# Attention and expert kernel: where slot 0's products on zeros stand, and where two additions of the front stand

## What is computed

```python
x = x + xattn(layernorm(x), ctx)      # 8 batches, 256 channels, 512 positions, 16 heads of 16 channels
x = x + ffn(layernorm(x))             # 2048 tokens of 512 numbers

# xattn
q = Wq @ x + bq; k = Wk @ c + bk; v = Wv @ c + bv
p = softmax(einsum('bhkt,bhks->bhts', q, k) * SCALE)
out = Wo @ einsum('bhts,bhks->bhkt', p, v) + bo

# ffn
h = rmsnorm(x) * rms_weight
probs = softmax(h @ router_w)                     # 8 experts, top 2 kept, their weights made to sum to 1
moe = sum over the two: weight * ((silu(h @ w_gate) * (h @ w_up)) @ w_down)
sh = (silu(h @ sw_gate) * (h @ sw_up)) @ sw_down  # the shared expert, for every token
return moe + sh
```

## Time and profile before

| | |
|---|---|
| device time, median of 3 runs | 826.72 us (823.37 to 827.68) |
| the profiled execution | 826.63 us on the device, span 824.8 us |
| TensorE matmul busy | 779.6 us (95%) |
| VectorE busy | 547.7 us (66%) |
| ScalarE busy | 419.8 us (51%) |
| GpSimd busy | 364.5 us (44%) |
| granted TensorE clock, mean | 0.993 of full |

### The profile page before, as it was taken

How to read it: one execution, slowest core, us unless ns; L and a number is a source line. 1 busy time by engine, 2 the same in 40 slices (tenths; PEclk the granted TensorE clock), 3 DMA queues, 4 the chain that set the end, 5 groups by cost and what they waited for, 6 DMA issues and landing times. The chain is left out here.

```text
span 824.8 us, 11865 instructions
## 1 busy us (share of the span) xinstructions
PE 779.6 (95%) x3879; PEld 393.6 (48%) x3879; DVE 547.7 (66%) x1048; ACT 419.8 (51%) x800; POOL 364.5 (44%) x309
## 2 busy tenths in 40 slices
PE   7999999989999999999999999998999999999993
PEld 3433334334334343343343455775546666666662
DVE  6687898898888888888888767587653223223231
ACT  2124667767768777687776674310343333333331
POOL 4154227417429246173222421000138777777774
PEclk9999999999999999999999999999999999999998
DMA  8959275567565765666543235510946665666553
GB/s 290 216 148 198 62 164 139 115 131 153 126 150 125 157 154 125 132 149 154 116 99 122 94 105 196 238 52 25 340 119 103 94 98 97 102 99 99 90 96 45
DMA packets 54186, 109.67 MB, mean 133 GB/s; under 512 B 12200, under 2 KB 27304, under 8 KB 49888
## 3 DMA queue, kind: packets, MB, share of 16 engines
q1 hardware_dynamic: 37080, 79.39, 38.5%
q0 software_dynamic: 16960, 29.37, 18.8%
q10 hardware_dynamic: 88, 0.16, 0.1%
HBM read 67.90 MB, written 40.86 MB: 132 GB/s over the span
## 5 line engine op out<-in xcount | busy, mean ns | idle before, releaser
L1090 DVE TENSOR_REDUCE negmax<-front_ps 128x1 f32<-128x512 f32 x512 | 326.9, 684 | 68.6 <-PE front_ps L932 67.4
L824 ACT ACTIVATE probs<-st_ps 128x512 f32<-128x512 f32 x512 | 284.0, 598 | 139.4 <-PE st_ps L968 139.1
L1376 POOL DMA_INDIRECT out<-ring,row_i x78 | 123.1, 1578 | 62.5 <-ACT ring L1432 46.4
L1607 PE MATMUL big_ps<-w_gu,attn 128*128 x244 | 111.3, 593 | 0.8 <-ACT attn L1425 0.8
L656 POOL CAST early<-early 128x512 fp32r<-128x512 f32 x28 | 17.1, 612 | 162.3 <-ACT early L772 158.1
L968 PE MATMUL st_ps<-stacks 50*128 50x512 f32 x256 | 68.5, 493 | 2.2 <-ACT probs L824 2.0
L1359 POOL DMA_INDIRECT ring<-h_rows,row_i x39 | 39.6, 1016 | 68.7 <-DMA out<-x_sb 57.1
L1446 ACT ACTIVATE attn<-big_ps 128x256 f32<-128x256 f32 x39 | 15.0, 384 | 106.1 <-PE big_ps L1607 106.1
L1816 DVE TENSOR_TENSOR zeros<-attn,big_ps 128x256 f32<-128x256 f32 x39 | 16.4, 421 | 78.6 <-ACT attn L1446 78.6
L981 PE MATMUL pv_ps<-probs,v_t 128*32 128x512 f32 x512 | 68.2, 605 | 0.5 <-ACT probs L824 0.5
L981 PE MATMUL pv_ps<-probs,early 128*32 128x512 f32 x512 | 68.2, 605 | 0.3 <-ACT probs L824 0.3
(11 more groups left out here) (218 smaller groups left out, 1218.4 us busy)
## 6 DMA issues: line engine op xcount, KB each, us to landing
parts_dram<-early SPq DMA_DIRECT2D x32, 512.0 KB, 3.9
stacks<-parts_dram SPq DMA_DIRECT2D x32, 256.0 KB, 5.4
w_gu<-in_gate_up SPq DMA_DIRECT2D x8, 1024.0 KB, 12.2
x_sb<-in_x SPq DMA_DIRECT2D x8, 512.0 KB, 12.2
early<-in_ctx POOLq DMA_DIRECT2D x8, 512.0 KB, 5.7
stacks<-parts_dram SPq DMA_DIRECT2D x32, 128.0 KB, 5.7
k_stack<-parts_dram SPq DMA_DIRECT2D x16, 256.0 KB, 5.0
q_stack<-parts_dram SPq DMA_DIRECT2D x16, 256.0 KB, 5.6
```

The source lines that it names most:

```text
L824: nc.scalar.activation(probs[:, k % 2, u % GH, :], score_bank(UNITS * s + u), ACT.Exp, scale=SCALE).then_inc(exp_done, 1)
L1090: nc.vector.tensor_reduce(negmax[:, n % 2, c:c + 1], smax_bank(UNITS * n + u), AX_X, ALU.max, negate=True).then_inc(max_done, 1)
L1376: nc.gpsimd.indirect_dma_start(outs[i], bass.IndirectOffsetOnAxis(ap=row_i[:, k:k + 1], axis=0), y_sb[:, k % RING, DY * i:DY * (i + 1)], N ...
L1607: mm = nc.tensor.matmul(gu_ps[:, :], h_t[:, k % 2, a, :], w_gu[:, bass.ds(expert, 1), a, :], start=(a == 0), stop=(a == DT - 1))
```

## The change

Slot 0: a product on zeros now stands ahead of the last maximum product of its pair, in the pairs u = 0, 2, 4, 6, 10 and 14, and is 384 columns wide. The pairs u = 8 and 12 have none. The front: `shared_add(2)` and `shared_add(3)` move from behind the running sum over tiles to behind `shared_act(3)`.

```diff
@@ TensorE, the loop over slots and units
                         while passed < maxima_until(s, u):
+                            if s == 0 and u < HALF_UNITS and (u < HALF_UNITS // 2 or u % GH > 0) and passed == maxima_until(s, u) - 1:
+                                pe.wait_ge(nm_parts_ready, 2)
+                                filler(proj_ps[:, 0:FILL])
                             max_pass(passed // UNITS, passed % UNITS)
                             passed += 1
...
-                        if s == 0 and u < HALF_UNITS:
-                            pe.wait_ge(nm_parts_ready, 2)
-                            filler(proj_ps[:, 0:T if u < HALF_UNITS // 2 else F])
@@ VectorE, the front
                 run = src
-                shared_add(2)
-                shared_add(3)
...
                 shared_act(3)
+                shared_add(2)
+                shared_add(3)
```

## The result

The changed kernel takes 821.8 us in the median of 20 executions, the kernel before 825.34 in 20 beside it. The ratio is 0.995, with a 95% interval from 0.9936 to 0.9964: 3 to 5 us faster. The forecast was 820.4, within 817.5 to 825.5. The profiled execution took 820.64, with a span of 818.7 against 824.8.

The account below looks back on a forecast made before the run. The kernel was taken as a long list of TensorE work, with time won where TensorE waits or works uselessly. Span 824.8 - 2.4 - 2.1 - 1.7 = 818.6, plus 1.8 on the device: 820.4 us, range 817.5 to 825.5.

Parts of the forecast that it names:

- a change of 0.5% would show: Whole kernel: faster by more than about 0.5% (4.1 us), that is below 822.6 us; chance 0.65.
- Slot 0: First eight pairs: zeros fill the 0.55 us wait before the fourth maximum product; 21.8 us becomes 19.4, gain 2.4.
- The front: VectorE's chain to the masks, L1761: two additions stop waiting 1.11 and 0.96 us, so all behind comes 2.07 earlier.
- The clock: TensorE behind L1761: with a wait of 0.4 instead of 2.46 us the clock stays full, gaining 1.7 us.
- Loads do not: Slot 0's gain is kept: loads have no clock of their own; the last lands at 67.0, first used at 74.6.
- Nothing reaches the end: Rival, block loop: queues and their landing set the pace, so the gains vanish; about 826 us, chance 0.07.
- The clock falls all the same behind L1761: Rival: half clock still comes there or near it, so only 4.5 us is gained; 822.1 us, chance 0.15.
- half clock at another place: Sign of a wrong prediction: the half clock appears somewhere other than behind L1761; no size given.
- Slot 0's gain is lost later: Rival: later work takes the gain back, or VectorE sets slot 0's pace more than reckoned; 822.8 us, chance 0.17.
- Slower: the clock falls in slot 0: Rival: fewer zeros let the clock drop to half through the eight pairs; 834 us, chance 0.06.

Follow-up runs that it names:

- slot 0's part: Only slot 0's part of the diff, put on the kernel before, with the front as before: ratio 0.9959 to the kernel before.
- TensorE busy in the wait: Kernel before plus eight products of 512 columns on TensorE ahead of its wait for the masks, into a bank nobody reads: ratio 0.9976.
- the front's part: Only the front's two moved additions, put on the kernel before, with slot 0 as before: ratio 0.9943 to the kernel before.
- the changed kernel's third: The changed kernel run a third time with nothing altered: ratio 0.9934 to the kernel before.

## Why the prediction was right

The mechanism came as told: zeros inside the wait, additions that no longer wait, TensorE's wait for the masks shortened. The number came in part by luck. The forecast subtracts 6.2 from the 826.6 of one execution. The gain of the medians was 3.5, and the kernel before has its median over twenty at 825.34. The sum was 2.7 too large and the start 1.3 too high, and so 820.4 lies 1.4 beside 821.8. That a change of 0.5% would show, to which I gave 0.65, is not borne out by this comparison: the ratio lies on that mark, and those of the two later ones, 0.9916 and 0.9934, below it.

**Slot 0, forecast 2.4, measured 2.8** in the eight pairs of the profile and 2.6 in the weighted span of the part alone. The forecast pairs, 1.96, 2.72, 3.48 and 1.96, were 1.74, 2.85, 3.95 and 1.74: the next scores start beside the last maximum product, 0.2 earlier than I reckoned, and the pair with a `pv` took 0.5 more. It was kept, in the main. From the first scores of slot 0 to L1498 behind the last slot, TensorE's timelines have, before and after:

```profile
505.58 1.08 PE L1498 MATMUL big_ps<-pv_raw,zeros 128*64 128x512 f32 x4 [0.45 <-PEq L540]
```

```profile
503.42 1.08 PE L1498 MATMUL big_ps<-pv_raw,zeros 128*64 128x512 f32 x4 [0.45 <-PEq L540]
```

That is 505.58 - 54.89 = 450.7 before and 503.42 - 55.63 = 447.8 after. The other profiles without a fall of the clock in that stretch give 449.8 and 450.0 with slot 0 as before (TensorE busy in the wait, and the front's part) and 447.9 for the changed kernel's third. So 1.9 to 2.9 are kept.

**The front, forecast 2.07, measured 2.16** in the profile and 2.2 for the part alone. TensorE's wait that is left is 0.83 and not 0.4, as TensorE is done with its own work 2.70 earlier (567.97 to 565.27), 0.5 more than the 2.16 by which L1498 came earlier; the reason is open.

**The clock, forecast 1.7, measured 1.61 in this pair of profiles, but it is the term that was mis-sized.** I took one profiled execution's fall for a fixed part of the kernel. It came in two of six; an estimate of its mean worth is some 0.5 by that count, and the mean clocks of one chip put it at up to 1.9. Other falls come at other places, in slot 0's pairs too. The span of the profiled pair fell by 6.1, close to the sum, but with 0.7 of chance in it: slot 0 began 0.74 later after (55.63 against 54.89), and from there on it is 6.8. The medians fell by 3.5 in the first comparison, 6.6 in the second and 5.2 in the third. The weighted spans, work and waits without the clock, fell by 3.8 to 4.9.

**What I drew from "Loads do not" left a store out**, without much effect on the number. I had looked at the loads that slot 0 needs, but not at what slot 0 itself sends next: its store of the maxima ran into the loads of x.

**The rivals.** "Nothing reaches the end" is out by both parts alone. "The clock falls all the same behind L1761" (822.1) is the nearest to the measured 821.8, but not by its mechanism: none of the four profiles with the changed kernel's lists there, the one with x loaded later among them, has a fall behind L1761. What I had named as a sign of being wrong, half clock at another place, did come in one of the four, in slot 0. "Slot 0's gain is lost later" is out for the most part, and true in single executions: by a wait of 0.17 in the first profile, and of 2.81 in that of slot 0's part. "Slower: the clock falls in slot 0" did not come as the usual course of this change, only as a single fall in one profile and perhaps in the execution of 845.9; that the danger was real is shown by the kernel without zeros. Why the clock falls at one place in one execution and at another in the next stays open.

## What to carry to other kernels

Work that is there only to keep TensorE busy belongs into the wait, ahead of the instruction that waits, not behind it: then the wait is used, and the work costs only what goes beyond it. How much of it is needed shows over many executions: with less of it or narrower, long executions came that the kernel before never showed. An addition that waits for a far engine should not stand in the middle of a chain of small steps that sets the end. Count a fall of the clock seen in one profile as a chance, and look at two or three executions before it goes into a sum; and when a stage gets faster, follow also what it sends to the queues.

## What the runs showed of the hardware

A wait of 2.46 us on TensorE, at the same place of the same front (slot 0 differs in three of the six), was followed by half clock in two profiled executions and by full clock in four. In one execution without the zeros the clock stayed at 0.50 for 44.5 us with TensorE busy 99% of them, in slot 0's mix of products on half of the array's rows and `pv`. A store of 32 KB that landed 1.5 us after its issue on quiet DMA engines took 3.4, 4.0 and 6.5 us behind 2 MB of loads.
